# Five rotating PSUM banks in the attention, own row buffers in FFN block 1, and half-by-half signals for masked scores

## The reference, cut to what matters

```python
x = x + xattn(layernorm(x), ctx_4096, ctx_4096, w_q, w_k, w_v, w_out, mask)
x = x + ffn(layernorm(x), w12, b12, w3, b3)
# xattn: scores = q @ k.T / sqrt(32); where(mask, scores, min); softmax; @ v; @ w_out.T
# ffn:   x1, x2 = split(x @ w12.T + b12); (silu(x1) * x2) @ w3.T + b3
```

## Time and profile before

| | |
|---|---|
| runs | 1094.68, 1098.26, 1099.54 us (median 1098.26) |
| profiled execution, its own time | 1090.49 us |
| its span, first to last instruction | 1088.6 us |
| mean granted TensorE clock | 0.987 |
| busy: PE / DVE / ACT / POOL | 95% / 63% / 39% / 46% |

### The profile page before, as it was taken

The page is one execution under the profiler, slowest core; times in us unless marked ns, Lnnn a source line. Parts: engine busy times, 40 slices in busy tenths (PEclk is TensorE's granted clock), DMA queues, the critical chain, the costliest instruction groups (busy, mean ns, idle before and its releaser), DMA issues.

```text
span 1088.6 us, 21832 instructions
## 1 busy us (share of the span) xinstructions
PE 1032.6 (95%) x8400; PEld 700.1 (64%) x8400; DVE 690.3 (63%) x2092; ACT 427.1 (39%) x967; POOL 495.4 (46%) x456
## 2 busy tenths in 40 slices
PE   7886999998998989999999999999999999999998
PEld 6775766866777667686655544444444788568853
DVE  6879888676776777668956623555866255734431
ACT  6756454544645445455465510113432011301110
POOL 3669701623636317247785959235864121203000
PEclk9998899999999999999999999999999999999999
DMA  9658598796898986669794661658549732784201
GB/s 376 234 136 158 126 248 205 195 239 186 193 261 207 218 213 147 176 156 226 178 269 106 128 232 67 223 149 301 207 152 230 266 116 69 185 235 138 83 1 78
DMA packets 230199, 199.11 MB, mean 183 GB/s; under 512 B 176976, under 2 KB 187216, under 8 KB 225232
## 3 DMA queue, kind: packets, MB, share of 16 engines
q1 hardware_dynamic: 230096, 197.72, 66.7%
HBM read 119.04 MB, written 35.65 MB: 142 GB/s over the span
## 4 chain that ended last, share of the span: by engine, by line
PE 61%; DVE 18%; DMA 5%; ACT 5%; issue 3%; POOL 2%; SPq 2%; DVEq 0%; ACTq 0%; POOLq 0%
PE bank_dense L1302 45%; PE bank_score L1447 11%; DVE arena_attn L1772 6%; DMA arena_rows<-w_t 4%; ACT arena_attn L1119 3%; DVE arena_in L1611 3%; PE bank_av L1447 3%; DVE arena_rows L1736 1%; SPq L672 1%; DVE small L1655 1%; DVE arena_attn L1741 1%; DMA arena_attn<-arena_attn 1%; DVE arena_rows L1666 1%; PE bank_score L1359 1%; ACT arena_rows L1083 1%
## 5 line engine op out<-in xcount | busy, mean ns | idle before, releaser
L1302 PE MATMUL bank_dense<-arena_rows,arena_in 128*128 128x256 f16 (+1 forms) x1920 | 263.0, 294 | 8.3 <-DVE arena_rows L1736 3.0
L1119 ACT ACTIVATE arena_attn<-arena_attn,arena_in 128x128 f32<-128x128 f32 x512 | 162.6, 390 | 204.7 <-DVE arena_in L1772 204.7
L1302 PEld LDWEIGHTS bank_dense<-arena_rows,arena_in 128*128 128x128 f16 x1920 | 185.4, 98 | 70.2 <-DVE arena_rows L1736 4.1
L901 POOL TENSOR_TENSOR arena_attn<-arena_attn 128x512 f16<-128x512 f32 x85 | 100.8, 1202 | 170.2 <-ACT arena_attn L1126 169.8
L1302 PE MATMUL bank_dense<-arena_out,arena_attn 128*128 128x512 f16 x768 | 170.6, 379 | 0.4 <-DVE arena_attn L1795 0.4
L1302 PE MATMUL bank_dense<-arena_attn,arena_rows 128*128 128x512 f16 x768 | 166.4, 379 | 0.0
L1772 DVE CUSTOM_DVE_ANT_0 arena_attn<-bank_score,arena_in 128x128 f32<-128x128 f32 x512 | 143.4, 345 | 0.4 <-POOL arena_attn L901 0.3
L1302 PEld LDWEIGHTS bank_dense<-arena_attn,arena_rows 128*128 128x128 f16 x768 | 75.1, 98 | 90.2
L1302 PEld LDWEIGHTS bank_dense<-arena_out,arena_attn 128*128 128x128 f16 x768 | 73.8, 98 | 84.8 <-DVE arena_attn L1795 0.6
L1302 PE MATMUL bank_dense<-arena_in 128*128 128x256 f16 x768 | 98.9, 291 | 4.5 <-DVE arena_attn L1741 2.2
L1302 PEld LDWEIGHTS bank_dense<-arena_in 128*128 128x128 f16 x768 | 79.0, 104 | 20.6 <-DVE arena_rows L1736 2.9
(11 more groups left out here) (173 smaller groups left out, 1599.1 us busy)
## 6 DMA issues: line engine op xcount, KB each, us to landing
arena_rows<-x SPq DMA_DIRECT2D x32, 512.0 KB, 6.0
arena_in<-w_scratch SPq DMA_DIRECT2D x64, 256.0 KB, 3.1
arena_attn<-q_scratch SPq DMA_DIRECT2D x48, 256.0 KB, 4.5
arena_rows<-w_t SPq DMA_DIRECT2D x12, 1024.0 KB, 6.4
arena_rows<-ctx_t SPq DMA_DIRECT2D x8, 1024.0 KB, 6.0
q_scratch<-arena_attn SPq DMA_DIRECT2D x16, 512.0 KB, 5.0
x_scratch<-arena_rows SPq DMA_DIRECT2D x16, 512.0 KB, 3.8
arena_out<-x_scratch SPq DMA_DIRECT2D x16, 512.0 KB, 6.0
```

The source lines that it names most:

```text
L901: ins = pool.tensor_tensor(p_split[:, g % 2, u, 1], e[:, g % 2, u], p_split[:, g % 2, u, 0], ALU.subtract)
L1119: ins = act.activation(head, head, ACT.Exp, bias=neg_max[:, g % 2, h:h + 1], scale=-1.0)
L1302: ins = pe.matmul(dst, lhs(a, c), rhs(b, c), start=(c == chunks[0] and n == 0), stop=(c == chunks[-1] and n == 2))
```

## The change

Three parts.

1. PSUM. There is one score pair left: `scores(g)` now waits until step g-1 was masked. The freed pair `bank_spare` gives two more banks to the rotation, from the first query product of block 1 until the last block's first output product (`FIVE`). Each product takes the bank that was filled longest ago, and waits for the read of that bank's last product; inside `FIVE` that is product n-5.
2. `mask_scores` signals after four heads and again after eight; `exps(g, 0)` waits for the first signal, `exps(g, 1)` for the second.
3. FFN. Row tiles 2 and 3 of block 1 have a buffer of their own (`y_next`, over the rows of FFN block 0), free when block 0's last hidden product is done. All four tiles are loaded, then all four turned, and `load_raw(0)` (which shares that place) waits for all four to be split; it and `load_raw(1)` stand behind the turns in SyncE's order. VectorE's order in block 0's output products is changed to suit. The last FFN block stores half rows, each behind its own output product.

```diff
+FIVE = range(DENSE[("q", 1, 0)], DENSE[("o", NB - 1, 0)])
+def banks():
+    held, n = {b: None for b in range(5)}, []
+    for i in range(len(DENSE)):
+        b = min(range(5 if i in FIVE else 3), key=lambda b: (-1 if held[b] is None else held[b], b))
+        n.append((b, held[b]))
+        held[b] = i
+    return n
+        y_next = part(arena_rows, 0, 8, F32).rearrange("p (r d) -> p r d", r=2)
-        B_SCORE = [stack.enter_context(nc.psum_tensor(f"bank_score{r}", [P, U * HALF], F32)) for r in range(2)]
+        B_SCORE, B_SPARE = (stack.enter_context(nc.psum_tensor(name, [P, U * HALF], F32))
+                            for name in ("bank_score", "bank_spare"))
+        B_ROTATE = [*(b[:, :] for b in B_DENSE), B_SPARE[:, 0:HALF], B_SPARE[:, HALF:]]
...
             def load_tile(r):
-                if late_tile(r):
+                if late_tile(r) and f < PLAIN:
+                    sp.wait_ge(s_dense, done("h", f - 1, MC - 1, 1))
+                elif late_tile(r):
                     sp.wait_ge(s_hid, MC * f)
...
-                elif n >= FT + 2:
-                    sp.wait_ge(s_rsplit, n - FT - 1)
...
             def load_raw(i):
-                if i < 2:
+                if i == 0:
+                    sp.wait_ge(s_rsplit, FT)
+                elif i == 1:
                     sp.wait_ge(s_dense, done("h", 0, MC - 1, 1))
...
-            load_tile(r)
-            load_tile(r + 1)
+            for u in range(FT):
+                load_tile(r + u)
+            for u in range(FT):
+                turn_tile(r + u)
             load_raw(0)
             load_raw(1)
-            turn_tile(r)
-            load_tile(r + 2)
-            turn_tile(r + 1)
-            load_tile(r + 3)
-            turn_tile(r + 2)
-            turn_tile(r + 3)
             store_out(0)
...
-                store_out(f)
                 if f + 1 < NF:
+                    store_out(f)
                     load_y_res(f + 1)
                 else:
+                    for q in range(8):
+                        h, u = q // FT, q % FT
+                        sp.wait_ge(s_dread, done("y", f, q))
+                        sp.dma_start(out_rows[FT * f + u][:, HALF * h:HALF * h + HALF], y_res[:, u, HALF * h:HALF * h + HALF])\
+                            .then_inc(s_out[u], 16)
...
             def exps(g, u):
-                if u == 0:
-                    act.wait_ge(s_neg, g + 1)
+                act.wait_ge(s_neg, U * g + u + 1)
...
             def begin(*key):
-                if n >= 3:
-                    pe.wait_ge(s_dread, n - 2)
+                if last is not None:
+                    pe.wait_ge(s_dread, last + 1)
+                elif n in FIVE:
+                    pe.wait_ge(*taken("v"))
...
-                if g >= 2:
-                    pe.wait_ge(s_neg, g - 1)
+                if g >= 1:
+                    pe.wait_ge(s_neg, U * g)
...
-                ins.then_inc(s_neg, 1)
+                    if h % HPG == HPG - 1:
+                        ins.then_inc(s_neg, 1)
...
             for q in range(8):
-                if q in (0, 1, 3, 4):
-                    row_stats(r + (q if q < 2 else q - 1))
-                if q in (1, 2, 4, 5):
-                    normalise(r + (q - 1 if q < 3 else q - 2))
-                if q in (2, 3, 5, 6):
-                    rows_lo(r + (q - 2 if q < 4 else q - 3))
+                if q < 2:
+                    row_stats(r + 2 * q)
+                    row_stats(r + 2 * q + 1)
+                    normalise(r + 2 * q)
+                    normalise(r + 2 * q + 1)
+                elif q < 6:
+                    rows_lo(r + q - 2)
                 ffn_residual(0, q)
```

More of the change, by code:

```diff
@@ L216 @@
 DENSE = {key: i for i, key in enumerate(dense_order())}
+FIVE = range(DENSE[("q", 1, 0)], DENSE[("o", NB - 1, 0)])
[6 more added lines that the diff above has]
+    return n
+BANKS = banks()
 def done(*key):
@@ L448, in late_tile @@
         def late_tile(r):
-            return r >= 2 * NB + PLAIN * FT and (r - 2 * NB) % FT >= 2
+            return r >= 2 * NB + FT and (r - 2 * NB) % FT >= 2
         def loaded(r):
@@ L1274, in begin @@
             def begin(*key):
-                n = DENSE[key]
+                n, last = DENSE[key], BANKS[DENSE[key]][1]
                 assert n == order[0], (key, n, order[0])
                 order[0] += 1
-                if n >= 3:
-                    pe.wait_ge(s_dread, n - 2)
+                if last is not None:
+                    pe.wait_ge(s_dread, last + 1)
+                elif n in FIVE:
+                    pe.wait_ge(*taken("v"))
                 return bank(*key)
@@ L1453, in idle_turns @@
                 for _ in range(n):
-                    pe.transpose(B_SCORE[1][:, HALF:HALF + P], ident[:, :], ident[:, :])
+                    pe.transpose(B_SPARE[:, HALF:HALF + P], ident[:, :], ident[:, :])
             pe.wait_ge(s_ident, 2)
```

20 lines of the change are left out of this document (10 added, 10 removed).

## The result

| | before | after |
|---|---|---|
| median of the runs, us | 1098.16 | **1064.97** (4 runs, 1063.87 to 1065.93) |
| profiled execution, its own time | 1090.49 | 1065.12 |
| its span | 1088.6 | 1063.3 |
| granted TensorE clock, mean of the runs (before: 32 runs beside the experiments) | 0.982 | 0.994 |

The ratio of after to before is 0.971, 95% interval 0.968 to 0.974: 33.2 us faster. 1074.8 was predicted, with a range of 1064 to 1087. The time lies in the range, near its lower end, and the sign was right. The terms were not all right, and the largest part of the difference is the clock. Every median, range and mean here leaves out two slow runs, one of the nineteen of the kernel before beside experiments 1 to 4 (1338.55 us) and one of the ten of kernel 4 (1772.19 us, granted clock 0.556).

What follows compares the result with a forecast made beforehand. TensorE, busy 95% of the span, was taken as the bound, its attention idle time (39.6 us) mostly waits for banks. Terms (a) to (i) summed to 23.5 us: 1098.26 - 23.5 = 1074.8 us, range 1064 to 1087.

Steps and rivals of the forecast that it cites:

- VectorE takes over: Rival, chance 0.17: a freed bank only moves the stall to VectorE's next debt; gain 8.2 us, time 1090.1.
- (c): Clock in blocks 1 to 6: fewer slow value products behind waits; gain 3.5 us, bounds nothing to 5.6.
- Time base: Sum made against the profiled execution's 1090.49 us; the same microseconds are subtracted from the median of 1098.26.
- (b): Last steps of blocks 2 to 6: bank waits shrink with five banks; gain 5 x 1.3 = 6.5 us.
- (a): Block 1: ScalarE starts after four heads, and the second value product gets its bank earlier; gain 3.3 us.
- (d): Waits for turned probabilities shrink because the transpose is issued about 0.95 us earlier; gain 1.9 us.
- (e): Block 6: the product that waits for the top's reduction has its bank free; gain 1.4 us.
- (f): Block 7: the wait for `divide` shrinks and three short bank waits go; gain 2.0 us.
- (g): Last step of block 7: `turn_attn`'s bank wait and the small wait behind it go; gain 2.3 us.
- (h): FFN block 1: earlier row tile loads remove the wait before its first product; gain 2.3 us.
- (i): The end: a last store of 256 KB instead of 512, size hardly counting; gain 0.3 us.
- the clock swings: Rival, chance 0.03: short waits stay and the clock falls between 132 and 560 us too; time 1095.

Runs made afterwards that it cites:

- experiments 1 to 4: Four runs against the kernel before: banks alone 1084.6 us, halves alone 1081.3, rows alone 1092.1, one score pair with nothing else changed 1098.6.
- kernel 4: The kernel before with one score pair, the freed pair unused and three dense banks: 1098.6 us, ratio 1.001.
- the second profile: The changed kernel run again, nothing altered: 1066.1 us.
- kernel 1: The kernel before with part 1 of the change only, five rotating banks and one score pair: 1084.6 us, ratio 0.987.
- kernel 7: The changed kernel without the fourth and fifth bank, two score pairs and three dense banks: 1083.8 us, ratio 0.988.
- kernel 5: The changed kernel without part 3, the row buffers and half-row stores: 1070.4 us, ratio 0.975.
- Kernel 8: kernel 1 with TensorE turning the identity ahead of the spread's wait, 40 times in blocks 1 to 6: 1081.3 us, ratio 0.985.
- kernel 10: The changed kernel with the spreads of steps 1 and 7 moved behind the step's second product: 1056.6 us, ratio 0.963.
- kernel 2: The kernel before with part 2 only, masked scores signalled by halves, two score pairs and three dense banks: 1081.3 us, ratio 0.985.

## Why the prediction was right, and where it was wrong

The mechanism was right in the main: the waits were waits for a bank, and they go. The spread's wait only changed its releaser (9.3 us, now 10.2 for the factors), which is part of what "VectorE takes over" said. In idle time the sum was 20.0 and the profiles show 16.9 (18.2 in the second profile). Three things stand between 1074.8 and 1065.0: 3.1 us of idle time less than forecast went, the clock gave 4.9 more between the profiles, and 7.9 more came from profile to median: 9.7 net. That the range held is in part luck: its lower end stands on "the highest bounds together (about 32 us)", and the bounds as given add up to 30.6. The 33.2 measured is above both, and lies in the range by the allowance for a repeat nearer the profiled time.

- **(c) clock, 3.5: the mis-sized term**, 8.4 in the profiles, above the bound of 5.6. I had counted 1.3 for each slow value product and two of three of them as mended. All three were (the second value products of blocks 2 to 6 take 2.78 to 2.79 in the changed kernel), and the slow stretch behind a wait holds more than that one product. By the windows' clock, 0.97 from 132 to 200 and 0.99 from 200 to 560 became 1.00, which is about 0.03 x 68 + 0.01 x 360 = 5.6 us, and 0.88 in block 1 became 0.91, 0.03 x 73 = 2.2; 7.8 of the 8.4.
- **Time base: "I subtract the same microseconds from the median" failed.** 32 runs of before spread over clocks of 0.978 to 0.987, with a mean of 0.982; each 0.001 goes with 1.1 us. Its profiled run, at 0.987, was at the best end. What the change mends of the clock, it mends more of in the usual run. The clocks of more than the one profiled execution would have shown what it did not hold, 0.005 or 5.5 us of slow products; that the change would mend them, no row said. (The 32 runs are of three chips; the 18 of one of them cover the whole spread.)
- **(b) last steps, 6.5**: too large for the banks alone (1.3 in block 2, 4.7 over the five steps in kernel 1), too small for the change. Halves shorten the same waits, and the pair leaves 0.7 to 1.1 of spread wait in blocks 2 to 5, 0.2 before block 2's value product, and nothing in block 6: of 12.9 us of waits in these steps 9.3 went. A plain block without a slow product, block 4, went from 68.6 to 66.1, 2.5.
- **(a) block 1, 3.3**: too large. Block 1 is 3.0 shorter, of which 1.5 is idle time (13.0 to 11.5) and 1.5 slow products, for which (c) had 0.9. The first step's 1.1 is exact. In the last step the first value product takes 2.78 instead of 5.30, and the spread then stands 4.53 for factors that come from VectorE.
- **(d) turned probabilities, 1.9: wrong.** The waits are 7.2 instead of 6.1. ScalarE's wait before the exponentials did shrink (from 204.7 to 126.4 in all, 78 against the 70 forecast), but TensorE arrives earlier too, by as much or more. I moved one side of this race and left the other where it was. Which of ScalarE, VectorE and DMA sets these waits now was not tried.
- **(e) block 6, 1.4**: right, no such wait is left; kernel 7, without the banks, has it (1.41).
- **(f) 2.0 and (g) 2.3**: (f) is right and belongs to halves. Of (g), the 2.06 for a bank went, and one of 0.93 for the low half of v took its place, at the row-tile turn behind the second value product; the wait at the first hidden product of block 8 grew from 0.57 to 1.26. Together 3.5 less 0.7, against 4.3. With halves alone the 2.06 grew to 3.91, so it is the banks that mend it.
- **(h) rows, 2.3**: right; 2.58 comes back in kernel 5. The later raw weights cost nothing, so that rival is out: there is no wait inside FFN block 1, though GpSimd's first sum starts 2.3 us ahead of the block's first product (703.43 and 705.72) where it was 10.9 ahead.
- **(i) end, 0.3**: about 0.5. From the last output's end on VectorE to the end of the span it was 3.12 us (1085.48 to 1088.6), and is 2.58:

```profile
1059.84 0.88 DVE L1884 SCALAR_TENSOR_TENSOR arena_out<-bank_dense,small,arena_out 128x256 f32<-128x256 f32 x2 [4.30 <-PE bank_dense L1327]
...
out<-arena_out SPq DMA_DIRECT2D x4, 512.0 KB, 2.6
...
out<-arena_out SPq DMA_DIRECT2D x8, 256.0 KB, 2.0
```

  "The size hardly counts" was wrong: in the last FFN block, where no other transfer runs beside them, the stores of 512 KB of before land in 2.6 us (middle row, its DMA issues from 1060 us on) and those of 256 KB of the changed kernel in 2.0 (lower row). Rows 8 hold medians over stores in crowded places. The rule of the Trainium skill ("DMA: Bandwidth & Descriptors", "Rules for kernel authors") to join many small transfers puts the overhead under 64 KB, so it does not bear on stores of this size; at the very end, where nothing else hides the landing, the smaller ones are better here.
- **The added wait, 0**: right (kernel 4).

Of the rivals, "the clock swings" was not only unlikely but the reverse of what came. The Trainium skill's rule ("TensorE: Matmul & The Clock Gate", "A second HAM failure mode: psum-queue depth-cycling") has the cycling through banks bring the clock down. Here more banks in the cycle, with halves, brought the mean from 0.982 to 0.994 (banks alone 0.984, which is within the scatter of before's runs). Kernel 8 points to the condition that the rule itself names, TensorE standing in short pieces: with some of them filled its mean grant is 0.990 against kernel 1's 0.984. The deeper rotation leaves less standing, not more. "VectorE takes over" holds for what is left: the waits for the factors were VectorE's, but kernel 10 shows that the place of the spread in the order of the programs made them count.

Still open: why kernel 7 (halves and rows) is 4 us above what was expected and not under kernel 2. Its idle time is 2.5 less than kernel 2's, and its clock 0.985 against 0.988, with four runs each, on two chips, that spread from 0.983 to 0.990. Open as well: how much of the gain of halves goes by VectorE's waits for weights, which no run separates.

## What to carry to other kernels

When an in-order engine waits for a buffer, look at whose program order releases it, and at whether the next thing in its own order could run instead: here a bank two places further back gave 8.8 us of idle time, a signal half a step earlier 7.6, and moving one tiny product behind a large one 6 to 7.5 more. Look also at what the late engine itself stood for: VectorE's waits for a load of weights (6.5 us) went with a signal that was meant for ScalarE. Read the granted clock of many runs before taking a profiled execution as the base, because short stands can cost twice, as idle time and as slow products behind them, and the second part varies from run to run.

## What the hardware showed unexpectedly

- The mean grant of one and the same program varies from run to run, 0.978 to 0.987, and its time with it, 1104 to 1092 us in 32 runs on three chips. The changed kernel's eight runs on two chips lie between 1063.9 and 1068.0, at 0.990 to 0.994.
- In these profiles a value product behind stands took up to 5.3 us instead of 2.8 (5.30 behind 2.19 and 4.09 behind 0.82, 1.28 and 0.40 in the kernel before); not every such stand was followed by one (2.79 behind 0.81 and 0.39 in kernel 1, 4.39 behind 1.24 and 0.39).
- With an identity turned while TensorE waits the mean grant was 0.990 against 0.984, and the time 3.3 us less, which is not clear of noise; VectorE's waits for loads of weights grew by 5.2 us in the same profile.
